# A Perceiver layer on one core: the feed-forward block's normalisation and rounding taken row tile by row tile, down weights shared between two engines, other banks for the transform

## What is computed

```python
x = x + _L0_attn_ref(_layernorm(x), ...)        # ends with out @ W_O
x = x + _L0_ffn_ref(_layernorm(x), w_gate, w_up, w_down)

def act_quant(x):                # per row
    scale = 128 / clip(max(abs(x), -1), 1e-5)
    return clip(round(x * scale), -128, 127) / scale
def weight_quant(w):             # ternary, one scale for the matrix
    scale = 1 / clip(mean(abs(w)), 1e-5)
    return clip(round(w * scale), -1, 1) / scale

gate = act_quant(x) @ weight_quant(w_gate).T     # 512 -> 2048
up = act_quant(x) @ weight_quant(w_up).T
u = silu(gate) * up
out = act_quant(fwht(u)) @ weight_quant(w_down).T  # Walsh-Hadamard over 2048
```

## Time and profile before

| what | value |
|---|---|
| median of three runs | 611.61 us |
| the profiled execution, time | 610.64 us |
| its span (first to last instruction) | 608.8 us |
| mean granted TensorE clock | 0.961 |
| TensorE busy | 544.0 us (89%) |
| VectorE busy | 450.4 us (74%) |
| ScalarE busy | 364.3 us (60%) |
| GpSimd busy | 38.2 us (6%) |

### The profile page before, as it was taken

One profiled execution on the slowest core, in us unless ns is written; L12 is line 12 of the kernel. 1 busy time (PEld: TensorE's weight loads), 2 busy tenths in 40 slices (PEclk: granted clock), 3 DMA queues, 4 the chain that ended last, 5 costly groups with the idle time before them and its releaser, 6 DMA issues. The chain is left out here.

```text
span 608.8 us, 10686 instructions
## 1 busy us (share of the span) xinstructions
PE 544.0 (89%) x4318; PEld 345.0 (57%) x4318; DVE 450.4 (74%) x846; ACT 364.3 (60%) x426; POOL 38.2 (6%) x30
## 2 busy tenths in 40 slices
PE   2999999998999899989987868799997999966696
PEld 1444555544566566656655555688883566532383
DVE  2599999956899999989997963112663885973974
ACT  4625566446899889989987982102126374737343
POOL 0300000002000200020020000000000000007200
PEclk9999999999999999999987988799999999996999
DMA  9623200052354344435552896000606605100000
GB/s 323 235 71 112 95 1 1 0 191 103 105 205 145 140 139 140 161 118 168 176 174 94 295 426 269 1 0 1 276 1 273 291 2 208 57 12 1 1 1 35
DMA packets 18897, 76.81 MB, mean 126 GB/s; under 512 B 1952, under 2 KB 3104, under 8 KB 16800
## 3 DMA queue, kind: packets, MB, share of 16 engines
q1 hardware_dynamic: 18848, 76.13, 34.8%
HBM read 75.34 MB, written 0.79 MB: 125 GB/s over the span
## 5 line engine op out<-in xcount | busy, mean ns | idle before, releaser
L1063 DVE CUSTOM_DVE_ANT_0 arena<-ps,arena 128x1024 f32<-128x1024 f32 x128 | 152.3, 1220 | 15.9 <-issue 9.1
L1436 ACT ACTIVATE arena<-arena,small 128x4096 int16<-128x4096 f32 x32 | 121.5, 3798 | 2.9 <-DVE small L1076 2.8
L576 PE MATMUL ps<-arena 128*128 128x512 f16 x384 | 100.1, 380 | 0.0
L617 PE MATMUL ps<-small,arena 128*128 128x128 bf16 x1024 | 83.6, 229 | 9.9 <-DVE arena L1083 4.8
L542 PE MATMUL ps<-arena 128*128 128x512 f16 x384 | 85.2, 379 | 1.2 <-DVE arena L994 1.2
L617 PEld LDWEIGHTS ps<-small,arena 128*128 128x128 bf16 x1024 | 62.9, 102 | 19.0 <-issue 6.5
L754 PE MATMUL ps<-arena 128*128 128x256 f32 (+1 forms) x288 | 70.0, 403 | 0.7 <-ACT arena L1513 0.7
L1443 ACT ACTIVATE arena<-ps 128x512 int32<-128x512 int32 x96 | 56.9, 592 | 20.8 <-PE ps L617 20.5
L754 PEld LDWEIGHTS ps<-arena 128*128 128x128 f32 x288 | 56.7, 197 | 12.2 <-issue 3.3
L542 PEld LDWEIGHTS ps<-arena 128*128 128x128 f16 x384 | 37.2, 98 | 43.6 <-issue 1.5
L633 PEld LDWEIGHTS ps<-arena 128*128 128x128 f16 x1024 | 42.8, 97 | 29.2 <-issue 4.5
(11 more groups left out here) (156 smaller groups left out, 745.6 us busy)
## 6 DMA issues: line engine op xcount, KB each, us to landing
arena<-key_scales SPq DMA_DIRECT2D x64, 512.0 KB, 4.8
arena<-in_ctxT SPq DMA_DIRECT2D x8, 1024.0 KB, 5.5
arena<-in_wg SPq DMA_DIRECT2D x1, 4096.0 KB, 12.0
arena<-in_wo SPq DMA_DIRECT2D x1, 4096.0 KB, 12.0
arena<-in_wu SPq DMA_DIRECT2D x1, 4096.0 KB, 22.0
arena<-in_wd SPq DMA_DIRECT2D x4, 1024.0 KB, 5.9
arena<-in_wuq SPq DMA_DIRECT2D x1, 3072.0 KB, 25.0
arena<-in_wkr SPq DMA_DIRECT2D x1, 2048.0 KB, 13.8
```

The source lines that it names most:

```text
L576: last = pe.matmul(ps[:, bank, :], wv16[wpart][:, k, g * P:(g + 1) * P], ctx16[cpart][:, k, tok], start=(k == 0 and i == 0), stop=(k == KC ...
L617: last = pe.transpose(ps[:, bank, :].bitcast(BF16)[:, b * P:(b + 1) * P], p16[u % 2][:, (8 * q + b) * P:(8 * q + b + 1) * P].bitcast(BF16) ...
L1063: dve.tensor_tensor_reduce(sc[:, u % 2, i * SCW:(i + 1) * SCW], ps[:, 2 * (n % 2):2 * (n % 2) + 2, :].rearrange("p a b -> p (a b)"), skb[: ...
L1436: act.activation(p16[u % 2], sc[:, u % 2, :], ACT.Exp, bias=ebias[:, u % 2:u % 2 + 1], scale=sq[:, i:i + 1], accum_out=rsum[:, u:u + 1]).t ...
```

## The change

Six edits, all in the stretch from 538 us on:

1. **Mean of the down weights sooner.** The matmul with ones moves from behind `project2(15)` to ahead of it, and VectorE reduces it ahead of the first residual.
2. **Row tile by row tile.** VectorE's chain from the residual to the rounded row runs to its end for t = 0, and then for t = 1, each with its own signals; ScalarE takes two square roots of 128x1; TensorE turns xi of t = 1 only after gate step 1.
3. **Function tables.** Two activations on one column, which nothing waits for, bring in the tables for Sqrt and Silu ahead of the first instruction that needs them.
4. **Down weights.** Chunks 0 and 1 are clipped and stored by VectorE, between `gated` 0 to 3 (the last store in the rounding of row tile 1); chunks 2 and 3 by GpSimd. ScalarE scales chunks 2 and 3 behind Silu 3 and Silu 4.
5. **Banks and place.** The turns and products of the transform go into banks 0 to 3, the gates' own, and wait for `ga` in place of `gd`; `uT` moves to another region, and ScalarE's wait for `gd` goes.
6. **Down product.** `down(0)` is cut in halves with `turn_ti(1)` between them; its bank becomes 4 + t.

```diff
@@ tensor: the loop over i, NH + 4 steps
+                if i == NH + 3:
+                    pe.wait_ge(wgs, 12)
+                    pe.wait_ge(as2, NH - 1)
+                    pe.matmul(ps[:, 4, N:N + 4], ones, wsum[:, 8:12], start=True, stop=True).then_inc(wdm, 1)
                 if 0 <= i - 4 < NH:
                     project2(i - 4)
-            pe.wait_ge(wgs, 12)
-            pe.matmul(ps[:, 4, N:N + 4], ones, wsum[:, 8:12], start=True, stop=True).then_inc(wdm, 1)
...
+            turn_xi(0)
             pe.wait_ge(tern, 24)
             for n in range(QT * 4):
                 if n == 0:
                     pe.wait_ge(xie, 1)
+                elif n == 2:
+                    turn_xi(1)
...
@@ tensor: hadamard and the turns ahead of it
-                    pe.wait_ge(gd, 7 + n)
+                    pe.wait_ge(ga, 7 + n)
-                    last = pe.matmul(ps[:, 6 + n % 2, b // 2 * N:(b // 2 + 1) * N], uT[:, n % 2, b, :],
+                    last = pe.matmul(ps[:, 2 + n % 2, b // 2 * N:(b // 2 + 1) * N], uT[:, n % 2, b, :],
...
-                        pe.wait_ge(gd, 5 + n)
+                        pe.wait_ge(ga, 5 + n)
-                        last = pe.transpose(ps[:, 4 + n % 2, b * P:(b + 1) * P], tt[1][:, t, a:a + P], id32[:, :])
+                        last = pe.transpose(ps[:, n % 2, b * P:(b + 1) * P], tt[1][:, t, a:a + P], id32[:, :])
...
-            for t in range(QT):
-                turn_ti(t)
-                down(t)
+            turn_ti(0)
+            down(0, range(IB // 2))
+            turn_ti(1)
+            down(0, range(IB // 2, IB))
+            down(1, range(IB))
@@ vector
-            variance(x1, residual2)
             dve.wait_ge(wdm, 1)
             link(dve.tensor_reduce(wmean[:, 2:3], ps[:, 4, N:N + 4], AX, ALU.add))
             mean_of(2, wmean[:, 2:3])
             dve.sem_inc(wdsc, 1)
...
             for t in range(QT):
+                link(residual2(t))
+                link(dve.bn_stats(stats[:, t, :], x1[:, t, :]))
+                link(dve.bn_aggr(mv[:, t, :], stats[:, t, :]))
+                dve.tensor_scalar(rstd[:, t:t + 1], mv[:, t, 1:2], EPS, None, ALU.add).then_inc(s_var, 1)
+                dve.wait_ge(s_std, 3 + t)
+                link(dve.reciprocal(rstd[:, t:t + 1], rstd[:, t:t + 1]))
...
                 clip(xi[:, t, :], xn3[:, t, :]).then_inc(xis, 1)
...
+            def clip_down(k):
+                dve.wait_ge(wdch, k + 1)
+                dve.tensor_scalar(wd32[k], wd32[k], MAGIC + 1.0, MAGIC - 1.0, ALU.min, ALU.max).then_inc(wdclip, 1)
+            def round_down(k):
+                dve.wait_ge(wdclip, k + 1)
+                dve.wait_ge(tern, 24)
+                dve.tensor_scalar(wdb[k], wd32[k], -MAGIC, None, ALU.add).then_inc(wdv, 1)
...
                     gated(4 * t + c)
+                    if t == 0 and c in (0, 2):
+                        clip_down(c // 2)
+                    elif t == 0 and c == 1:
+                        round_down(0)
...
+                    if t and n == 1:
+                        round_down(1)
@@ gpsimd
-            for k in range(4):
+            for k in (2, 3):
...
@@ scalar
+            act.activation(exp_table[:, :], id32[:, 0:1], ACT.Sqrt)
+            scale_down(0)
+            std_row(0)
+            scale_down(1)
+            store_xiT(0)
+            std_row(1)
+            act.activation(exp_table[:, :], id32[:, 0:1], ACT.Silu)
             for n in range(QT * 4):
...
+                if n == 1:
+                    store_xiT(1)
+                elif n in (3, 4):
+                    scale_down(n - 1)
...
-                act.wait_ge(gd, min(7 + n, 8))
```

More of the change, by code:

```diff
@@ L235, in build @@
         junk = at(rest + 15872, [WCH])
-        uT = at(rest + 19968, [2, 4, P])
+        uT = at(o_tail + 32768, [2, 4, P])
         tiT = at(rest, [IB, N], BF16)
@@ L863, in hadamard, with down @@
                 else:
-                    pe.wait_ge(gd, 7 + n)
+                    pe.wait_ge(ga, 7 + n)
                 for b in range(4):
-                    last = pe.matmul(ps[:, 6 + n % 2, b // 2 * N:(b // 2 + 1) * N], uT[:, n % 2, b, :],
+                    last = pe.matmul(ps[:, 2 + n % 2, b // 2 * N:(b // 2 + 1) * N], uT[:, n % 2, b, :],
                                      had_sb[:, b % 2 * P:(b % 2 + 2) * P], start=(b % 2 == 0), stop=(b % 2 == 1))
                 last.then_inc(hp, 1)
-            def down(t):
+            def down(t, blocks):
                 if t == 0:
-                    pe.wait_ge(wdr, 4)
-                for b in range(IB):
+                    pe.wait_ge(wdv, 2)
+                    pe.wait_ge(wdr, 2)
+                for b in blocks:
                     if b % 8 == 0:
                         pe.wait_ge(*((tid, 1) if t and b else (tie, 2 * t + b // 8 + 1)))
-                    last = pe.matmul(ps[:, 2 + t, :], tiT[:, b, t * P:(t + 1) * P],
+                    last = pe.matmul(ps[:, 4 + t, :], tiT[:, b, t * P:(t + 1) * P],
                                      wdb[b // 4][:, (b % 4) * D:(b % 4 + 1) * D], start=(b == 0), stop=(b == IB - 1))
-                last.then_inc(dn, 1)
+                if blocks[-1] == IB - 1:
+                    last.then_inc(dn, 1)
             def turn_ti(t):
@@ L1281, in _ @@
             dve.sem_inc(wdsc, 1)
-            normalize(x1, xn3, 2)
-            dve.wait_ge(s_xn, 3 * QT)
             for t in range(QT):
[L1285 to L1291, removed]
-                clip(xi[:, t, :], xn3[:, t, :]).then_inc(xis, 1)
-            for a in range(2):
-                ins = dve.tensor_scalar(deq[:, a, :], amax[:, :], wmean[:, a:a + 1], None, ALU.mult)
-            link(ins)
-            dve.sem_inc(wum, 1)
+                link(residual2(t))
[4 more added lines that the diff above has]
+                link(dve.reciprocal(rstd[:, t:t + 1], rstd[:, t:t + 1]))
+                link(dve.tensor_scalar(xn3[:, t, :], x1[:, t, :], mv[:, t, 0:1], rstd[:, t:t + 1],
+                                       ALU.subtract, ALU.mult))
+                link(dve.tensor_reduce(amax[:, t:t + 1], xn3[:, t, :], AX, ALU.max, apply_absolute_value=True))
+                scales_of(slice(t, t + 1))
+                link(to_units(xn3[:, t, :], t))
+                clip(xi[:, t, :], xn3[:, t, :]).then_inc(xis, 1)
+                for a in range(2):
+                    ins = dve.tensor_scalar(deq[:, a, t:t + 1], amax[:, t:t + 1], wmean[:, a:a + 1], None, ALU.mult)
+                link(ins)
+                dve.sem_inc(wum, 1)
+            def clip_down(k):
[5 more added lines that the diff above has]
+                dve.tensor_scalar(wdb[k], wd32[k], -MAGIC, None, ALU.add).then_inc(wdv, 1)
             def gated(n):
@@ L1354, in _ @@
                                        ALU.add).then_inc(vint, 1)
-            pool.wait_ge(wum, 1)
-            for k in range(4):
+            for k in (2, 3):
                 pool.wait_ge(wdch, k + 1)
-                pool.tensor_scalar(wd32[k], wd32[k], MAGIC + 1.0, MAGIC - 1.0, ALU.min, ALU.max).then_inc(wdclip, 1)
-            for k in range(4):
-                pool.wait_ge(wdclip, k + 1)
-                pool.wait_ge(tern, 3 * (KC + (3 if k < 2 else 4)))
+                pool.tensor_scalar(wd32[k], wd32[k], MAGIC + 1.0, MAGIC - 1.0, ALU.min, ALU.max).then_inc(wdpc, 1)
+                pool.wait_ge(wdpc, k - 1)
+                pool.wait_ge(tern, 24)
                 pool.tensor_scalar(wdb[k], wd32[k], 1.0, -MAGIC, ALU.mult, ALU.add).then_inc(wdr, 1)
@@ L1558, in _, with std_row, store_xiT @@
             act.wait_ge(ones_s, 2)
-            std(2)
-            for k in range(3):
-                scale_down(k)
-            act.activation(junk[:, 0:1], ones[:, 0:1], ACT.Silu).then_inc(achain, 1)
-            act.wait_ge(achain, 1)
-            for t in range(QT):
+            def std_row(t):
+                act.wait_ge(s_var, 3 + t)
+                act.activation(rstd[:, t:t + 1], rstd[:, t:t + 1], ACT.Sqrt).then_inc(s_std, 1)
+            def store_xiT(t):
                 act.wait_ge(xit, t + 1)
@@ L1568, in _ @@
                                ACT.Copy).then_inc(xie, 1)
-            scale_down(3)
-            act.wait_ge(wum, 1)
+            act.activation(exp_table[:, :], id32[:, 0:1], ACT.Sqrt)
[5 more added lines that the diff above has]
+            act.activation(exp_table[:, :], id32[:, 0:1], ACT.Silu)
             for n in range(QT * 4):
+                if n % 4 == 0:
+                    act.wait_ge(wum, n // 4 + 1)
                 act.wait_ge(gp, n + 1)
```

9 lines of the change are left out of this document (5 added, 4 removed).

## The result

The changed kernel took 605.82 us (median of 8 runs, 604.74 to 607.97), the kernel before 611.23 us (8 runs, 609.02 to 614.25). The ratio is 0.9917, 95% interval 0.9891 to 0.9943: faster by 3.5 to 6.7 us, 5.1 in the middle. The forecast was 608.9, 2.7 us less than the 611.61 that it started from: the sign is right and the time inside the range, but the gain is about twice the forecast's. Two of the experiments' profiled executions (e2_pool_late, e7_all_on_pool) were disturbed, and nothing is read from their traces.

The account below looks back on a forecast made before the run. From 538 us on, a relay of waits between engines, with no busy engine, bounds the kernel. Terms -6.0 + 6.1 - 2.3 - 0.2 = -2.4 us, taken as -2.7, give 608.9 us; range 603.2 to 611.2.

Parts of the forecast that it names:

- terms 1 to 3: Residual to butterflies of tile 0: earlier mean, separate row tiles, early tables, chunks 0 and 1 on VectorE; 6.0 us gained.
- term 4: Butterflies of tile 0: GpSimd's four operations on chunks 2 and 3 take turns with them; 6.1 us lost.
- term 5: Last butterfly of tile 0 to turns of tile 1: new banks and uT; 2.3 us gained, up to 3.1.
- term 6: Tail: down(0) cut in halves around the turns lets down(1) start sooner; 0.2 us gained, 0 to 0.5.
- the gates (548): Sign in the new profile that the forecast is right: gates start near 548 us, 554.56 before.
- the butterflies (559.3): Sign in the new profile that the forecast is right: butterflies of tile 0 start near 559.3 us, 565.28 before.
- my limit of 549.5: Sign for the front: it is wrong if the first gate matmul comes after 549.5 us.
- The first turn: Sign at the transform's start: TensorE's first turn stands 1.1 us ahead of the last butterfly's end.
- A: Butterflies of tile 0: VectorE keeps its lead, GpSimd gets in only at two stage ends; 605.7 us, chance 0.27.
- B: Butterflies of tile 0: GpSimd gets nothing while VectorE has work; 603.6 us, chance 0.17.
- D: Front: tiles do not come sooner, scale_down(0) stands ahead of ScalarE's square root; 610.5 us, chance 0.07.
- C: Transform of tile 0: TensorE stays at half clock after its longer pause; slower, 616.4 us, chance 0.06.

Follow-up runs that it names:

- e2: Changed kernel with GpSimd's two chunks waiting for the last butterflies of row tiles 0 and 1; 599.78 us, ratio 0.9797.
- e7_all_on_pool: Changed kernel with all four chunks clipped and stored by GpSimd, behind the rounding of row tile 1; 607.59 us, ratio 0.9913.
- e5: Changed kernel with VectorE's chain over both row tiles at once and one square root; 609.05 us, ratio 0.9959.
- e6: Changed kernel without the two activations that load the function tables ahead; 608.29 us, ratio 0.9958.
- e1: Changed kernel with GpSimd's four operations on 128 of 2048 columns, half of the down weights left out of the result; 598.02 us, ratio 0.9767.
- e9: Changed kernel with each of GpSimd's four operations cut into two of 128x1024; 606.13 us, ratio 0.9894.
- e10: The same program as e2, GpSimd's chunks behind the butterflies, run again to read its trace; 601.25 us, ratio 0.9839.
- e3: Changed kernel with the edit of banks and uT undone, old waits for gated back; 609.50 us, ratio 0.9969.
- e4: Changed kernel with the down product of row tile 0 whole again ahead of the turns of tile 1; 606.90 us, ratio 0.9937.
- e8: Kernel before with only the change of banks and uT, the down product's bank with it; 607.65 us, ratio 0.9950.
- e11: Changed kernel with down weights off GpSimd: VectorE clips chunks 2 and 3 between butterfly stages, ScalarE stores them; 602.41 us, ratio 0.9851.

## Why the prediction was right, and where it was short

1. *Front (terms 1 to 3).* Forecast: butterflies 17.7 us behind the first residual; measured 17.77. e5 and e6 show its parts, 2.7 us for taking the row tiles apart and 1.8 for the tables; the mean was not undone alone. That the size is met to 0.1 us is partly luck. I had written that the gates' half clock costs nothing, since VectorE would be the later one. It wasn't: two products waited for the Silus, 0.33 and 0.53 us. In e1, where none waited, the same stretch took 16.81 us, so VectorE's own work was put 0.9 us too long, and the half clock made up for that.
2. *GpSimd against the butterflies (term 4).* Right in mechanism, shown by the traces of e1, e9 and e10, with e2's time in line. Mis-sized: 6.1 us forecast as lost, 5.2 measured. I put 1.9 + 1.2 us on a pair of turns. GpSimd's operations start 2.83 us apart (564.74, 567.57, 570.40), 0.3 less.
3. *Turns (term 5).* 2.3 us forecast, 3.26 measured. This is the other mis-sized term, and it comes from the order within term 4. I had all four of GpSimd's operations ahead of the fifth butterfly. GpSimd came 0.05 us behind the second one (561.73 against 561.68; 0.02 to 0.05 us in the other traces with the same order, e3 to e6 and e9), so the fourth fell behind the fifth, and the turns that need only this one started 2.7 us ahead of gated(4) and not 1.1. TensorE's half clock (back by 575) was then hidden, which e5 shows to be partly chance (9.19 where the clock came back later), and VectorE's fifth butterfly of tile 1 became the bound, which I had named as the limit of the gain (8.9 us; 8.83 measured).
4. *Down product (term 6).* 0.2 forecast, 0.2 measured, 0.3 by e4.

From the first residual on, the forecast's terms come to 17.7 - 23.9 + 6.1 - 2.3 - 0.2 = -2.6 us (and I leaned 0.3 further), and -4.4 was measured. Of the 1.8 us missing, 0.9 are term 4 and 0.9 term 5. The medians differ by 5.4 us, 1.0 more than the stretch shows; that is inside the interval and the scatter of the first residual, and no run here separates it. The two profiled executions differ by less, 3.1 us (610.64 and 607.56), since the changed kernel's first residual stood 1.4 us later.

Of the signs that I had set, the gates (548) and the butterflies (559.3) came at 549.2 and 560.54, both late by the 1.2 us by which the first residual was (542.77 against 541.6). The gates' record at 549.58 is over my limit of 549.5, but it has 15 of 16 matmuls and the weight load at 549.17 belongs to the missing one. The first turn stood 2.8 us ahead of the last butterfly's end, where I had 1.1, and the long butterflies were 2.8 to 2.9 us and not 3.1: these two are the sizes missed in terms 5 and 4.

Of the rivals, A (GpSimd gets in at stage ends only) hit the time, 605.7 us, by another way: the rows at 565.66 and 571.32 are butterflies within a stage and waited like the others. B and D are refuted by the same timeline, C by the clock's return before 575. That A's time was met is no support for A.

## What to carry to other kernels

A wait of VectorE and GpSimd for each other is recorded as busy time: an operation that is longer than its kind by what is left of another engine's operation is a wait in disguise, and the ends of both records show it. Before moving work to GpSimd, list what VectorE runs beside it; it was free beside products that read PSUM and beside maxima, and cost 1.6 us per operation beside butterflies, more than VectorE would have spent doing it. And bring front work forward only after asking what then meets on the new schedule: here 5 of the 6 us gained at the front were lost to a collision, and one semaphore wait (e2, e10) brought most of them back.

## What was not expected

- GpSimd and VectorE alternate by operation and not by size: 2.8 us per butterfly against whole operations of 1.9 us, 2.0 against halves.
- In a contested pair the cycle is 2.83 us, 0.3 less than the two alone.
- Nearly equal pauses of TensorE ended differently: 2.58 us in e8 with the clock still full and the first product at 1.99 us, 2.80 us in e11 with the clock down at about 570.6 (the mean of 0.78 in that stretch) and the product at 3.78. In the kernel before, a pause of 3.94 us ended with the clock still full: 1.00 over the first turns (574.58 to 575.80) and 0.50 from 576 on.
